# An image-token transformer block: the value projection's high and low weights side by side, in two banks

## The chip, the cores and the metric

The kernel runs on one core of one Trainium2 chip. The metric is the device time of one launch in microseconds (us). The text uses the engines' names: TensorE (PE in the rows; PEld for its weight loads), VectorE (DVE), ScalarE (ACT), GpSimd (POOL) and SyncE (SP), whose queue issues most transfers.

## What is computed

For each of 64 images of 3 x 224 x 224 a patch embedding with position codes, three layers of a graph convolution over a 28 x 28 grid and an output projection give 784 tokens of 64 features; 77 text tokens are joined to them, so that an image has 861 tokens. Then come attention with four heads of 16 features and a mixture of four experts, both behind a normalisation. Cut to what matters here:

```python
h = concatenate([tokens(x), txt], axis=1)                 # 64 x 861 x 64
a = layernorm(h)
q, k, v = heads(a @ Wq.T + bq), heads(a @ Wk.T + bk), heads(a @ Wv.T + bv)
out = softmax(q k^T / 4) v                                # per image and head
h = h + bf16(out) @ Wo.T + bo
h = h + shared_mlp(layernorm(h)) + top-2 of 4 experts, weighted
```

## The kernel before, in words

**Order of the work.** Everything after the setup is one list of steps (`window`, `image_steps`, `pair_steps`, lines 83 to 235). Each step has a due time in units of an image; all engines walk through the same list, sorted by due time, and each issues what its own branch of the step says. Work of several images overlaps: in the unit from g to g + 1 the scores of image g are formed (steps `s`, line 1121, and `pv`, line 1130), while the maxima of image g + 1 (`mx`, TensorE line 1142, VectorE line 894) and the experts of image g - 1 are worked on. `spread` divides the time between a start and an end over steps by their `COST`. The tables at lines 163 to 178 hold the starts and ends, one pair for even and one for odd images: `FINISH` (transposes of the attention output, line 1217, emptied at lines 995 and 996, and the output projection), `NORM_M` (normalisation ahead of the experts: its sum is line 946, its scaling line 965), `VALUE` (the value projection), `PACK`, `FETCH` and `LOAD_LEAD` (loading and packing of image columns, for SP and GpSimd) and more. The work of the graph convolution (`gw`, line 1169, low parts on VectorE at line 916; `gagg`, line 1178) is done for a pair of images, in the first half of each even unit. So a pair of images, an even and an odd one, is the period of the schedule. Sixteen pairs are laid out as one program window; the engines meet between windows.

**Banks.** PSUM has eight banks. Two hold the attention output (`pv`). The other six (0, 1, 2, 3, 6, 7) rotate: each step in `ROTATING` takes the next one, TensorE waits until the step six turns earlier has been emptied by its reader (semaphore `free`), and the reader waits for `full`. Each engine works in the order of the list, so a step that VectorE reads late holds its bank, and the turn six later waits on TensorE.

**Precision.** Weights and activations of some products are split into a high and a low part in fp32r. The token stack `x_stack_attn` (XS["a"], 128 rows: 64 features high, 64 low; 861 columns) is made by step `xt`. A product with the high weights (WH) and one with the low weights (WL), added in PSUM, give the value at nearly full precision.

**The value projection** (step `v`, TensorE lines 1198 to 1212, VectorE lines 982 to 989). An image has NB = 7 blocks of BLK = 123 tokens. For each block the tokens' 128 x 123 tile is the stationary operand, and the 64 columns of the value weights are streamed twice, high and low, into the same 64 columns of one bank:

```python
for k in range(NB):
    x_ = XS[which][:, k * BLK:(k + 1) * BLK]
    for part in (WH, WL):
        mm = pe.matmul(T[0:BLK, k * HID:(k + 1) * HID], x_, wsplit(part, "v"),
                       start=part is WH, stop=part is WL)
```

VectorE then adds the bias to all 7 x 64 columns in one operation and writes `v_and_one` (VV, two images deep), which the first `pv` of that image waits for. The gate's projection (step `gate`, line 1207) has its high and low weights side by side already, as `gate_hi_lo`. Semaphore `v_chain` orders VectorE's dependent operations (`done`, `need`, `settle`).

## Time and profile before

| | |
|---|---|
| times of three runs | 5132.30, 5137.61, 5141.29 us, median 5137.61 |
| the profiled execution | 5131.56 us, span 5129.8 us |
| mean granted TensorE clock | 0.968 of full speed |
| instructions in the span | 81306 |
| products and weight loads | 29710 each |
| DMA | 386.00 MB, mean 75 GB/s |

The first value projection starts some 235 us into the span: until then the setup, the first images' loading and the first graph layers run. The last stretch has the last images' experts. Between them the schedule repeats with each pair of images, and the two program windows that it fills differ little. In a row of the time line, a run of like instructions is merged: its start, the time from its first start to its last end, and behind it in brackets the idle time of the engine ahead of it and what ended that. A weight load of TensorE can run beside the product before it. The durations of products hold their latency, so their distance from start to start is shorter than the duration.

### The profile page before, as it was taken

The numbers are of one execution on the slowest core, as the hardware profiler recorded it, in microseconds if no ns is written. First come the engines' busy times: TensorE is split into PE (matmuls) and PEld (weight loads), VectorE is DVE, ScalarE is ACT, GpSimd is POOL, SyncE is SP. The second block draws the span as 40 slices with busy tenths as digits, with TensorE's granted clock in tenths as the row PEclk, the third lists the DMA queues.
The fourth block names the chain that finished last, engine by engine and source line by source line (L and its number), as shares of the span: only waits on it lengthen the run. The fifth ranks groups of instructions, "written<-read, shape, count | busy, mean of one in ns | idle before, by whom it ended". The sixth has DMA issues, their size and how long they took to land.

```text
span 5129.8 us, 81306 instructions
## 1 busy us (share of the span) xinstructions
PE 4804.8 (94%) x29710; PEld 3194.6 (62%) x29710; DVE 3517.5 (69%) x7660; ACT 2991.8 (58%) x6161; POOL 1268.7 (25%) x1169
## 2 busy tenths in 40 slices
PE   5389999999999999999999999999999999999998
PEld 4256666666666666666666666666666666666654
DVE  3167677777777776777776777777677777767774
ACT  0036666656666665666665665666566666666665
POOL 1113122222222222222221222222222222222121
PEclk8689999999999999999999999999999999999998
DMA  1332333343333243334333333324323332332220
GB/s 38 102 89 73 84 80 72 77 88 80 77 85 70 75 86 82 79 77 85 72 79 77 79 79 86 73 74 86 82 79 78 86 73 77 86 82 70 39 46 6
DMA packets 193397, 386.00 MB, mean 75 GB/s; under 512 B 74986, under 2 KB 118634, under 8 KB 193002
## 3 DMA queue, kind: packets, MB, share of 16 engines
q1 hardware_dynamic: 191978, 379.91, 33.2%
q8 instruction: 240, 3.93, 0.4%
q14 instruction: 155, 1.27, 0.1%
q10 hardware_dynamic: 1024, 0.89, 0.1%
HBM read 309.13 MB, written 109.26 MB: 82 GB/s over the span
## 4 chain that ended last, share of the span: by engine, by line
PE 55%; issue 22%; POOL 10%; DVE 6%; ACT 3%; DMA 2%; SPq 0%; POOLq 0%; ACTq 0%; DVEq 0%; another core or an unknown queue 0%
PE ps L1142 9%; PE ps L1121 8%; PE ps L1130 8%; PE ps L1178 8%; PE ps L1196 5%; PE ps L1169 4%; DVE neg_max_halves L894 3%; PE ps L1239 3%; POOL tokens L746 3%; POOL moe_T L741 2%; ACT probs L778 2%; PE ps L1260 2%; DMA image_rows<-image_by_row 2%; PE ps L1154 2%; POOL nodes_T L723 1%
## 5 line engine op out<-in xcount | busy, mean ns | idle before, releaser
L894 DVE TENSOR_REDUCE neg_max_halves<-ps 123x1 f32<-123x432 f32 (+1 forms) x3584 | 2016.6, 597 | 596.4 <-PE ps L1142 586.8
L778 ACT ACTIVATE probs<-ps 123x432 f32<-123x432 f32 x3584 | 1684.3, 541 | 602.2 <-PE ps L1121 579.8
L1142 PE MATMUL ps<-k_stack,q_stack 96*123 96x432 f32 x3584 | 1299.9, 396 | 37.3 <-DMA k_stack<-qk_scratch 22.3
L1121 PE MATMUL ps<-q_stack,k_stack 97*123 97x432 f32 x3584 | 1247.0, 394 | 64.5 <-DVE neg_max_halves L894 22.1
L1142 PEld LDWEIGHTS ps<-k_stack,q_stack 96*123 96x123 f32 x3584 | 644.1, 188 | 432.4 <-issue 289.5
L1121 PEld LDWEIGHTS ps<-q_stack,k_stack 97*123 97x123 f32 x3584 | 642.8, 186 | 360.2 <-issue 96.6
L1130 PE MATMUL ps<-probs,v_and_one 123*32 123x432 f32 x7168 | 787.7, 553 | 13.8 <-ACT probs L778 13.8
L841 ACT ACTIVATE hidden<-ps,plain_w 128x432 f32<-128x432 f32 x640 | 400.5, 634 | 182.0 <-PE ps L1196 181.9
L1178 PE MATMUL ps<-adjacency,parts_hi 112*128 112x392 f32 x1344 | 467.0, 347 | 5.3 <-DVE parts_lo L916 4.1
L1178 PE MATMUL ps<-adjacency,parts_lo 112*128 112x392 f32 x1344 | 461.7, 344 | 0.0
L711 POOL COPY patch_columns<-image_rows 96x392 f32<-96x392 f32 x256 | 238.3, 959 | 822.5 <-PE ps L1154 736.0
L1130 PEld LDWEIGHTS ps<-probs,v_and_one 123*32 123x32 f32 x7168 | 183.8, 111 | 373.6 <-issue 272.7
L727 POOL TENSOR_TENSOR ln_stats_m<-ln_stats_m,minus_half 123x7 f32<-123x7 f32 x64 | 95.1, 1485 | 1242.9 <-DVE ln_stats_m L960 1242.9
L741 POOL TENSOR_TENSOR moe_T<-gate_weights,bias_rows 123x448 f32<-123x448 f32 x256 | 254.1, 993 | 394.8 <-DVE gate_weights L1064 356.7
L723 POOL TENSOR_TENSOR nodes_T<-nodes_T,dinv_row 128x392 f32<-128x392 f32 x128 | 130.9, 1023 | 883.9 <-ACT nodes_T L790 883.9
L746 POOL TENSOR_TENSOR tokens<-tokens,moe_T 123x448 f32<-123x448 f32 x256 | 292.6, 1143 | 33.0 <-POOL moe_T L741 0.9
L1169 PE MATMUL ps<-plain_w,nodes_T 128*112 128x128 f32 (+2 forms) x1792 | 250.3, 279 | 31.4 <-POOL nodes_T L723 28.3
L785 ACT ACTIVATE parts_hi<-ps 112x512 fp32r<-112x512 f32 x192 | 104.9, 546 | 284.4 <-PE ps L1169 284.3
L847 ACT ACTIVATE hidden<-ps,plain_w 128x492 f32<-128x492 f32 (+1 forms) x384 | 234.1, 636 | 62.5 <-PE ps L1239 52.1
L1178 PEld LDWEIGHTS ps<-adjacency,parts_hi 112*128 112x128 f32 x1344 | 256.5, 191 | 18.3 <-DVE parts_lo L916 12.0
L1178 PEld LDWEIGHTS ps<-adjacency,parts_lo 112*128 112x128 f32 x1344 | 256.7, 191 | 1.4
L933 DVE TENSOR_TENSOR nodes_T<-ps,dinv_row 128x392 f32<-128x392 f32 x192 | 108.4, 565 | 209.7 <-PE ps L1178 207.6
(156 smaller groups left out, 6197.9 us busy)
## 6 DMA issues: line engine op xcount, KB each, us to landing
image_rows<-image_by_row SPq DMA_DIRECT2D x256, 586.9 KB
q_stack<-qk_scratch SPq DMA_DIRECT2D x256, 216.0 KB, 8.2
k_stack<-qk_scratch SPq DMA_DIRECT2D x256, 216.0 KB, 9.3
image_by_row<-in_x SPq DMA_DIRECT2D x192, 196.0 KB
qk_scratch<-parts_hi SPq DMA_DIRECT2D x64, 432.0 KB, 2.5
qk_scratch<-parts_lo SPq DMA_DIRECT2D x64, 432.0 KB, 3.2
out<-tokens SPq DMA_DIRECT2D x64, 215.2 KB
tokens_next<-in_txt SPq DMA_DIRECT2D x64, 19.2 KB
```

The costliest lines, as they stand in the source:

```text
L711: pool.tensor_copy(XCB[:, b, :, :].rearrange("p g (i j) -> p g i j", j=GRID), src).then_inc(xc_done, 1)
L741: ins = pool.tensor_tensor(TMP[:, :, :], GW[:, :, e:e + 1].to_broadcast(shape), row("eb3", e).unsqueeze(1).to_broadcast(shape), ALU.mult)
L746: ins = pool.tensor_tensor(hb, hb, TMP[:, :, :], ALU.add)
L778: act.activation(P[:, (g * 2 * NB + unit) % SLOTS, h, :], T[0:BLK, 0:HW], ACT.Exp, scale=SCALE).then_inc(free[r], 1)
L841: act.activation(H1[e % 3][:, c0:c0 + cn], T[:, 0:cn], ACT.Relu, bias=bias).then_inc(free[r], 1)
L894: v.tensor_reduce(NM[:, qb * HEADS + h, half:half + 1], T[0:BLK, 0:keys], AX.X, ALU.max, negate=True).then_inc(free[r], 1)
L1121: mm = pe.matmul(T[0:BLK, 0:cn], KS[:, g % 2, h, kb * BLK:(kb + 1) * BLK], QS[:, g % 2, h, c0:c0 + cn], start=True, stop=True)
L1130: pm = pe.matmul(acc[32 * h:32 * h + 32, half, 0:HW], VV[:, g % 2, kb, h, :], P[:, slot, h, :], start=kb == 0, stop=kb == NB - 1, tile_pos ...
L1142: mm = pe.matmul(T[0:BLK, 0:cn], QS[0:SHIFT_ROW, g % 2, h, qb * BLK:(qb + 1) * BLK], KS[0:SHIFT_ROW, g % 2, h, c0:c0 + cn], start=True, st ...
L1169: mm = pe.matmul(T[0:m, at * 128:(at + 1) * 128], HT[:, k * size:k * size + m], rhs, start=True, stop=True)
L1178: mm = pe.matmul(T[:, 0:GHALF], part[:, k, :], adj[:, k, half * GHALF:(half + 1) * GHALF], start=k == 0 and part is UH, stop=k == NG - 1 a ...
L1196: mm = pe.matmul(T[:, 0:cn], wsplit(part, name, e, cols), XS[which][:, c0:c0 + cn], start=part is WH, stop=part is WL)
```

## The change

The value weights' high and low parts are copied once, in the setup, into one tile of 128 columns (`v_hi_lo`). Each block now has one product of 128 columns, so that the high half and the low half lie side by side in PSUM. 7 x 128 columns don't fit into a bank of 512, so the step becomes two, `("v", g, 0)` with blocks 0 to 3 and `("v", g, 1)` with blocks 4 to 6, each with a bank and a turn of its own; the second is due VGAP = 0.163 after the first. VectorE adds bias and high half, and then, behind a wait on its own semaphore, the low half, for each of the two. The first product with the values waits for both. The cost of `v` goes from 7 to 3, and due times of `FINISH`, `NORM_M`, `BIAS`, `PROJECT`, `VALUE`, `PACK`, `FETCH` and `LOAD_LEAD` are changed. The gate's branch is written anew and does what it did.

```diff
--- before.py
+++ after.py
@@ -80,7 +80,7 @@
 STACK_PARTS = 8
 SLOTS = 3
 WAIT = 9
-COST = {"s": 1, "pv": 4, "mx": 1, "embed": 5, "gw": 5, "gagg": 12, "xt": 2, "qk": 2, "v": 7, "gate": 4, "l1": 2,
+COST = {"s": 1, "pv": 4, "mx": 1, "embed": 5, "gw": 5, "gagg": 12, "xt": 2, "qk": 2, "v": 3, "gate": 4, "l1": 2,
         "l2": 4, "wt": 2, "wb": 1, "l3": 12, "ot": 4, "obt": 2, "wo": 6, "back": 4, "mrow": 2}
 
 
@@ -161,21 +161,22 @@
 
 
 MAX = ((-0.693, 0.158), (-0.638, 0.167))
-FINISH = ((1.016, 1.084), (1.072, 1.145))
-NORM_M = ((1.109, 1.222), (1.167, 1.195))
+FINISH = ((1.002, 1.07), (0.994, 1.145))
+NORM_M = ((1.109, 1.222), (1.154, 1.195))
 EXPERT = ((1.374, 1.997), (1.267, 1.882))
 GATE = ((1.464, 1.665), (1.347, 1.379))
-BIAS = ((1.602, 1.743), (1.585, 1.71))
+BIAS = ((1.602, 1.743), (1.572, 1.71))
 NORM_A = ((-1.472, -1.34), (-1.672, -1.474))
-PROJECT = ((-1.307, -1.271), (-1.361, -1.284))
+PROJECT = ((-1.307, -1.281), (-1.361, -1.284))
 STACK = ((-1.043, -1.0), (-1.082, -0.936))
-VALUE = (-1.012, -0.998)
+VALUE = (-0.962, -0.984)
 
 GRAPH = (-2.077, -1.521)
-PACK = (-4.063, -3.676, -3.424, -2.795)
+PACK = (-4.053, -3.676, -3.424, -2.795)
+VGAP = 0.163
 STORE = (2.555, 2.602)
-FETCH = -5.76
-LOAD_LEAD, EMBED_LAG = 0.144, 0.217
+FETCH = -5.73
+LOAD_LEAD, EMBED_LAG = 0.133, 0.217
 
 
 def image_steps(g):
@@ -191,7 +192,7 @@
             + part(norm_steps(g, "m"), NORM_M) + part(expert_steps(g), EXPERT) + part(gate_steps(g), GATE)
             + part([("hb", g, n) for n in range(2 * EXPERTS + 1)], BIAS) + part(norm_steps(g, "a"), NORM_A)
             + part(project, PROJECT) + part([("stack", g, n) for n in range(STACK_PARTS)], STACK)
-            + [(g + VALUE[b], ("v", g)), (g + STORE[b], ("store", g))])
+            + [(g + VALUE[b], ("v", g, 0)), (g + VALUE[b] + VGAP, ("v", g, 1)), (g + STORE[b], ("store", g))])
 
 
 def pair_steps(p):
@@ -306,6 +307,7 @@
         ident_bf = sb("ident_bf", [128, 128], BF16)
         before = sb("before", [128, 16], F32)
         gsplit = sb("gate_hi_lo", [128, 2 * EXPERTS], F32R)
+        vsplit = sb("v_hi_lo", [128, 2 * HID], F32R)
         selcol = sb("expert_columns", [128, EXPERTS], F32)
         wo3 = sb("wo_parts", [65, 3, 64], BF16)
         posb = sb("pos_and_bias", [128, PATCHES], F32)
@@ -403,6 +405,8 @@
                     settle(v.tensor_tensor(WL[:, :], raw[:, :], WH[:, :].bitcast(F32), ALU.subtract))
                     v.tensor_copy(gsplit[:, 0:EXPERTS], wsplit(WH, "gW").bitcast(F32))
                     v.tensor_copy(gsplit[:, EXPERTS:2 * EXPERTS], wsplit(WL, "gW").bitcast(F32))
+                    v.tensor_copy(vsplit[:, 0:HID], wsplit(WH, "v").bitcast(F32))
+                    v.tensor_copy(vsplit[:, HID:2 * HID], wsplit(WL, "v").bitcast(F32))
                     sel = slice(SEL_ROW, SEL_ROW + 3 * EXPERTS)
                     settle(v.tensor_tensor(selcol[sel, :], ident[sel, SEL_ROW:SEL_ROW + EXPERTS],
                                            ident[sel, SEL_ROW + EXPERTS:SEL_ROW + 2 * EXPERTS], ALU.add))
@@ -980,13 +984,16 @@
                                                in1=QKH[:, c0:c0 + cn].bitcast(F32), op0=ALU.add, op1=ALU.subtract
                                                ).then_inc(free[r], 1)
                     elif kind == "v":
-                        b = st[1] % 2
+                        _, g, part = st
+                        ks = blocks_of(part)
+                        k, kn = slice(ks[0][0], ks[-1][0] + 1), len(ks)
                         v.wait_ge(full[r], n)
-                        v.tensor_tensor(
-                            VV[:, b, :, :, 0:HD],
-                            T[0:BLK, 0:NB * HID].rearrange("p (k h d) -> p k h d", h=HEADS, d=HD),
-                            row("bv").rearrange("p (h d) -> p h d", h=HEADS).unsqueeze(1)
-                            .to_broadcast([BLK, NB, HEADS, HD]), ALU.add).then_inc(free[r], 1)
+                        two = T[0:BLK, 0:kn * 2 * HID].rearrange("p (k a h d) -> p k a h d", a=2, h=HEADS, d=HD)
+                        bias = row("bv").rearrange("p (h d) -> p h d", h=HEADS).unsqueeze(1).to_broadcast([BLK, kn, HEADS, HD])
+                        done(v.tensor_tensor(VV[:, g % 2, k, :, 0:HD], two[:, :, 0, :, :], bias, ALU.add), st)
+                        need(st)
+                        v.tensor_tensor(VV[:, g % 2, k, :, 0:HD], two[:, :, 1, :, :], VV[:, g % 2, k, :, 0:HD], ALU.add
+                                        ).then_inc(free[r], 1)
                     elif kind == "ot":
                         ks = out_blocks(st[2])
                         k0, kn = ks[0], len(ks)
@@ -1123,7 +1130,8 @@
                     elif kind == "pv":
                         _, g, half, kb = st
                         if (half, kb) == (0, 0):
-                            emptied(pe, turn, ("v", g))
+                            emptied(pe, turn, ("v", g, 0))
+                            emptied(pe, turn, ("v", g, 1))
                         emptied(pe, turn, ("s", g, half, kb, HEADS - 1))
                         slot = (g * 2 * NB + half * NB + kb) % SLOTS
                         for h in range(HEADS):
@@ -1195,21 +1203,16 @@
                         for part in (WH, WL):
                             mm = pe.matmul(T[:, 0:cn], wsplit(part, name, e, cols), XS[which][:, c0:c0 + cn],
                                            start=part is WH, stop=part is WL)
-                    elif kind in ("v", "gate"):
-                        g = st[1]
-                        which = "a" if kind == "v" else "m"
-                        if kind == "gate":
-                            emptied(pe, turn, ("xt", g, "m", 0))
-                            emptied(pe, turn, ("xt", g, "m", 1))
+                    elif kind == "gate":
+                        emptied(pe, turn, ("xt", st[1], "m", 0))
+                        emptied(pe, turn, ("xt", st[1], "m", 1))
                         for k in range(NB):
-                            x_ = XS[which][:, k * BLK:(k + 1) * BLK]
-                            if kind == "gate":
-                                mm = pe.matmul(T[0:BLK, k * 2 * EXPERTS:(k + 1) * 2 * EXPERTS], x_, gsplit[:, :],
-                                               start=True, stop=True)
-                                continue
-                            for part in (WH, WL):
-                                mm = pe.matmul(T[0:BLK, k * HID:(k + 1) * HID], x_, wsplit(part, "v"),
-                                               start=part is WH, stop=part is WL)
+                            mm = pe.matmul(T[0:BLK, k * 2 * EXPERTS:(k + 1) * 2 * EXPERTS],
+                                           XS["m"][:, k * BLK:(k + 1) * BLK], gsplit[:, :], start=True, stop=True)
+                    elif kind == "v":
+                        for k, at in blocks_of(st[2]):
+                            mm = pe.matmul(T[0:BLK, at * 2 * HID:(at + 1) * 2 * HID],
+                                           XS["a"][:, k * BLK:(k + 1) * BLK], vsplit[:, :], start=True, stop=True)
                     elif kind == "ot":
                         _, g, part = st
                         emptied(pe, turn, ("pv", g, part, 0))
```

## Rows read from the trace of the kernel before

**Rows 1.** The page, busy time of each engine with its share and instructions.

```profile
PE 4804.8 (94%) x29710; PEld 3194.6 (62%) x29710; DVE 3517.5 (69%) x7660; ACT 2991.8 (58%) x6161; POOL 1268.7 (25%) x1169
```

**Rows 2.** Steady stage: us; busy PE, PEld, DVE, ACT, POOL (instructions); clock, DMA share, GB/s.

```profile
3000.00:4000.00 1000.00, 972.77 (x6104) 647.12 (x6106) 718.90 (x1564) 615.62 (x1270) 256.87 (x238) 0.99 0.36 80
```

**Rows 3.** The page, the chain that ended last, share of the span.

```profile
PE 55%; issue 22%; POOL 10%; DVE 6%; ACT 3%; DMA 2%; SPq 0%; POOLq 0%; ACTq 0%; DVEq 0%; another core or an unknown queue 0%
```

**Rows 4.** Waits of the weight loads in 3000 to 4000: in total, times, longest.

```profile
PEld ps L1121 <- DVE neg_max_halves L894: 17.1, 53, 0.8
PEld ps L1121 <- ACT probs L778: 15.0, 33, 0.9
```

**Rows 5.** Line 1211 alone: duration in ns min/median/max, first and last start.

```profile
L1211 PEld LDWEIGHTS ps<-split_hi,x_stack_attn x448: 182/188/330, 235.7 to 4967.0; 128*123 128x123 f32 x150
```

**Rows 6.** Instructions in order: start, duration of the run, engine, line (four groups of products).

```profile
4152.41 0.27 PE L1211 MATMUL ps<-split_lo,x_stack_attn 128*123 128x64 f32 x1
...
4153.70 0.27 PE L1211 MATMUL ps<-split_lo,x_stack_attn 128*123 128x64 f32 x1
...
3094.72 0.60 PE L1265 MATMUL ps<-ident_r,moe_T 128*123 128x128 f32 x4
...
3046.12 0.81 PE L1207 MATMUL ps<-gate_hi_lo,x_stack_moe 128*123 128x8 f32 x7
```

**Rows 7.** VectorE's groups: shapes, count | busy us, mean ns | idle before.

```profile
L985 DVE TENSOR_TENSOR v_and_one<-ps,bias_rows 123x448 f32<-123x448 f32 x64 | 39.4, 616 | 17.9 <-PE ps L1211 17.9
L946 DVE TENSOR_REDUCE ln_stats_m<-tokens 123x7 f32<-123x448 f32 x64 | 39.4, 615 | 0.1
...
L996 DVE TENSOR_TENSOR attn_bf<-ps,inv_sums 123x256 bf16<-123x256 f32 x64 | 27.2, 424 | 2.2
L1094 DVE TENSOR_TENSOR tokens<-ps,tokens 123x256 f32<-123x256 f32 x64 | 26.6, 416 | 16.0 <-PE ps L1265 16.0
L996 DVE TENSOR_TENSOR attn_bf<-ps,inv_sums 123x192 bf16<-123x192 f32 x64 | 22.9, 358 | 2.2
L1095 DVE TENSOR_TENSOR tokens<-ps,tokens 123x192 f32<-123x192 f32 x64 | 22.3, 348 | 0.0
...
L995 DVE RECIPROCAL inv_sums<-ps 123x16 f32<-123x16 f32 x64 | 16.1, 252 | 0.3
```

**Rows 8.** Instructions in order, an even image's value step at 4152.

```profile
4151.59 3.17 DVE L894 TENSOR_REDUCE neg_max_halves<-ps 123x1 f32<-123x429 f32 x6 [1.18 <-PE ps L1142]
...
4154.81 0.40 PEld L1217 LDWEIGHTS ps<-ident_r,attn_T 128*123 128x123 f32 x3 [0.33 <-DVE neg_max_halves L894]
...
4159.29 1.12 DVE L894 TENSOR_REDUCE neg_max_halves<-ps 123x1 f32<-123x432 f32 x2 [0.29 <-PE ps L1142]
```

**Rows 9.** Stretches of 5 us, columns as in rows 2.

```profile
4068.00:4073.00 5.00, 5.00 (x34) 4.95 (x34) 3.29 (x8) 1.33 (x3) 0.00 (x0) 1.00 1.06 124
...
4153.00:4158.00 5.00, 4.90 (x28) 3.41 (x26) 4.93 (x13) 2.48 (x5) 0.00 (x0) 1.00 1.04 120
4158.00:4163.00 5.00, 4.94 (x53) 3.18 (x53) 3.92 (x9) 3.19 (x6) 0.00 (x0) 1.00 1.04 113
...
4168.00:4173.00 5.00, 4.47 (x31) 2.52 (x29) 4.93 (x11) 3.71 (x8) 0.90 (x1) 1.00 0.14 40
```

**Rows 10.** Instructions in order, after the even image's value step, 4164 to 4171.

```profile
4164.97 0.18 PEld L1121 LDWEIGHTS ps<-q_stack,k_stack 97*123 97x123 f32 x1 [0.89 <-ACT probs L778]
...
4166.78 1.30 DVE L965 TENSOR_TENSOR centred_and_squared<-centred_and_squared,ln_stats_m 123x448 f32<-123x448 f32 x1 [1.60 <-POOL ln_stats_m L727]
...
4169.77 1.11 DVE L894 TENSOR_REDUCE neg_max_halves<-ps 123x1 f32<-123x432 f32 x2
...
4170.43 0.46 PE L1121 MATMUL ps<-q_stack,k_stack 97*123 97x432 f32 x1 [0.53 <-DVE neg_max_halves L894]
```

**Rows 11.** Instructions in order, after the odd image's value step at 4067.8.

```profile
4072.47 0.57 DVE L933 TENSOR_TENSOR nodes_T<-ps,dinv_row 128x392 f32<-128x392 f32 x1 [1.71 <-PE ps L1178]
...
4085.24 0.19 PEld L1178 LDWEIGHTS ps<-adjacency,parts_hi 112*128 112x128 f32 x1 [0.38 <-DVE parts_lo L916]
```

## The prediction

> **What bounds the kernel now.** I read the page's engine table first, then a table by stages, then the chain, the waits, and last the order of instructions around the two places that the change touches. TensorE is busy 4804.8 of 5129.8 us and VectorE 3517.5 [rows 1]. In a steady stage of 1000 us TensorE is at 973, VectorE at 719 and ScalarE at 616, at a granted clock of 0.99 of 2.4 GHz [rows 2]. The chain that ended last is 55% TensorE and 22% issue [rows 3]. So the kernel is bound by TensorE, but not at every moment: in that same stage the weight loads of the score products wait 17.1 us for VectorE's maxima and 15.0 us for ScalarE's exponentials [rows 4], as a new product may only start when one of six rotating banks is empty. The value projection runs 64 times, its first start at 235.7 us and the start of its last block at 4967.0 us [rows 5], which makes (4967.0 - 235.7) / 63 = 75.1 us for an image; this is also the length of one unit of due time.
>
> **What is removed from TensorE.** An image has 14 products of 64 columns now. From the second to the fourteenth start of one group it is 4153.70 - 4152.41 = 1.29 us for 12 steps, 0.1075 us each [rows 6], so 14 cost 1.51 us. The new product has 128 columns and the same stationary tile of 123. No row shows just that; the nearest are four fp32 products of 128 columns on 123, which take (0.60 - 0.27) / 3 = 0.11 us each (0.27 being the last one's own duration, taken from the value products), and seven of 8 columns on 123, (0.81 - 0.27) / 6 = 0.09 us [rows 6]. Eight, 64 and 128 columns cost about the same: the stationary tile sets the pace. I take 0.109 us: 7 products cost 0.76 us. TensorE is relieved of 0.75 us an image, 48 us in 64 images. The TensorE page of the Trainium skill (TensorE: Matmul & The Clock Gate, Back-to-back issue gap) speaks against the change: it counts some 60 cycles for up to 64 columns and 134 for 128. By it alone, 7 x 134 against 14 x 60 cycles, TensorE would pay 0.04 us more for each image; the row of the products of 128 columns is against that, and the rule is a rival below.
>
> **What is added to VectorE.** Now one addition of 448 elements takes 616 ns. The two parts have 256 and 192 elements and two additions each. Additions of these sizes from a bank take 416 and 348 ns, and a dependent one starts some 34 ns after the one before it (2.2 us over 64) [rows 7]. So part 0 costs 2 x 0.416 + 0.03 = 0.86 us, part 1 0.73 us, together 1.59 against 0.62: 0.97 us more an image, 62 us in all. This would be more than TensorE gains, were VectorE the bound; it counts only where VectorE has no idle time left.
>
> **Even images, part 0** (due 0.05 later than now, some 4 us; the finish of the image before is 0.014 earlier). Here VectorE starts six maxima at 4151.59 and next waits for TensorE at 4159.29, for 0.29 us; TensorE waits for a bank in between (0.33 us ahead of the transposes, the first of three such waits) [rows 8]. In 4153 to 4158 VectorE is busy 4.93 of 5 us, in 4158 to 4163 3.92 [rows 9]. Taking 1.51 us out of TensorE's queue here and putting 0.44 us back (4 x 0.109) gives at most 1.07 us. VectorE gets 0.86 - 0.62 = 0.24 us more in 10 us in which it has 5 + 5 - 4.93 - 3.92 = 1.15 us free, and that leaves at most 0.91 us. The lower end is a loss of 0.24 us, if its queue sets the pace throughout. I take a gain of 0.45 us, between the ends, as the first half of the stretch is full and the second isn't.
>
> **Even images, part 1** (0.163 after part 0, due 1.201). By the due times it falls between score products, at about 4165. There TensorE waits 0.89 us for ScalarE already [rows 10], and 3 x 0.109 = 0.33 us of products cost nothing; should that wait be gone, they cost 0.33 us. On VectorE the new step stands behind the scaling of the normalisation (line 965, due 1.193), which waits 1.60 us for GpSimd and starts at 4166.78. Behind it come the high and low parts, then the first maxima at 4169.77, and for these TensorE waits 0.53 us at 4170.43 [rows 10]. The 0.73 us are put into exactly this queue, in a window where VectorE is at 4.93 of 5 us [rows 9]. So the cost is between 0 (part 0 and the finish bring all of it forward) and 0.73 us; I take 0.50 us. An even image then comes out at about -0.45 + 0.50 = +0.05 us.
>
> **Odd images.** The window is full for TensorE (5.00 of 5) and not for VectorE (3.29) [rows 9]: after the value step it waits 1.71 us for the first aggregation [rows 11]. Part 0, and the two transposes that the new finish times (0.994 for 1.072) put ahead of that aggregation, can use this idle time: 0.24 us for part 0, and the four operations that empty the transposes, 1.28 us together (twice 0.25 at most, 0.42, 0.36 [rows 7]), are 1.52 us. The transposes also fill TensorE while it would wait for the low parts, so they cost nothing where they go, and their 1.1 us is missing where they were. The gain is 1.07 us. Part 1, due 0.179, goes ahead of an aggregation that waits 0.38 us for line 916 [rows 11]: 0.33 us of products fit. But the normalisation now starts at 0.154 in place of 0.167, ahead of that line 916 (due 0.157), and its first sum takes 0.62 us (line 946, [rows 7]): between 0 and 0.62 us are lost; I take 0.22 us, since the wait covers some. An odd image: -1.07 + 0.22 = -0.85 us, with ends of -1.07 and -0.45 us.
>
> **The small ones.** Two casts of 64 columns in the setup, once: less than two of the 0.62 us additions [rows 7], and at nothing, as TensorE counts the graph's edges beside them; uncovered 1.2 us. PACK, PROJECT, FETCH and LOAD_LEAD move their steps by 0.010 to 0.030, 0.8 to 2.3 us. SP's fetches and loads and GpSimd's packing go past a few stacks and score steps with them; a fetch is due 1.07 images, 80 us, before its first load, and GpSimd is at 257 of 1000 us [rows 2], so nothing; if a packing is late in each pair its embedding waits at most 0.8 us, 26 us in all. The wait of the first product with the values for part 1 is 0.8 of an image later than part 1, and covered. One more turn of the banks for each image comes at the price already counted, the bank held behind VectorE. The first and last 200 us are not counted.
>
> **The sum.** A pair of images: -0.85 + 0.05 = -0.80 us; 32 pairs: -26 us. The profiled execution took 5131.6 us, which becomes 5106; the median of the runs shown is 6 us above that execution, and against it I say 5111.
>
> **Rivals.** (1) **TensorE sets the pace everywhere**: -0.75 us x 64 = -48 us, from the median 5090; with part 1 hidden in waits, -1.07 x 64 = -68 us, 5069. For it is the busy share of 97%; against it are the waits of rows 8 and 10. (2) **The odd images' gain is eaten by the even ones**: even part 0 gives nothing and part 1 costs its 0.73 us; -0.85 + 0.73 = -0.12 us, -4 us, 5134. For it: VectorE is at 4.93 of 5 us at both even places. (3) **VectorE's queue becomes the bound** at the first maxima after the normalisation: even images lose 0.24 + 0.73 = 0.97 us, and odd ones lose their gain, as the transposes and part 0 (1.52 us) overrun the 1.71 us of idle time once this has shrunk by the 1.07 us that TensorE is earlier, and part 1 and the earlier sum cost 0.22 us net: +1.19 us a pair, +38 us, 5176. It decides once the maxima are later by more than the finish is earlier. Against it: VectorE is at 72% over the stage. (4) **A product of 128 columns costs twice one of 64**: 7 x 0.215 us are the 1.51 us of now, nothing is gained, and VectorE's terms (0.05 + 0.45 on even, 0.22 on odd images) stay: +0.72 us a pair, +23 us, 5161. This is the page's rule as rows price it. The 0.11 us of rows 6 speak against it.
>
> **The numbers.** My forecast 0.47, rival 1 0.25, rival 2 0.14, rival 3 0.11, rival 4 0.03. A measurement of this kernel can tell about 0.2% (10 us) from no change, so faster means under 5127, slower over 5148. Faster: the forecast, rival 1 and a little of rival 2's spread, 0.73; the same: rival 2, 0.13; slower: rivals 3 and 4, 0.14. The range leaves out rivals 3 and 4 and the far end of rival 1: 5078 to 5138.
>
> **What would show it.** In the profile after: products of line 1211's successor at 0.107 to 0.112 us from start to start (0.2 would be rival 4); VectorE's additions x256 of about 416 and 348 ns; TensorE's busy time lower by some 50 to 60 us; the wait for the first maxima in rows 10 longer by half a us on even images and none such on odd ones; distances between the odd and the next even value step shorter, and the other distance the same. Wrong I would be if the even images gain as much as the odd ones, or if waits for line 894 grow by over 1 us an image.

## The result, and the profile after

The changed kernel takes 5109.83 us (median of six runs, 5105.71 to 5111.67) against 5134.95 us for the kernel before (median of six, 5129.94 to 5141.29): a ratio of 0.9949 with a 95% interval of 0.9936 to 0.9961, or 25 us less. The forecast was 5111 us. The rest of this document shows that most of the gain of the profiled execution did not come the way that the forecast had it.

First the page of the changed kernel: busy time of each engine, and the chain that ended last.

```profile
PE 4797.5 (94%) x29262; PEld 3164.6 (62%) x29262; DVE 3520.8 (69%) x7854; ACT 3002.0 (59%) x6161; POOL 1268.7 (25%) x1169
...
PE 55%; issue 23%; POOL 8%; DVE 8%; DMA 3%; ACT 2%; SPq 0%; POOLq 0%; ACTq 0%; DVEq 0%; another core or an unknown queue 0%
```

Compared with [rows 1] and [rows 3], the weight loads are fewer by 448 (7 an image) as they should be, but TensorE's busy time fell by 7.3 us only, and VectorE's rose by 3.3 us, not by the 62 us that the forecast added. Next, the changed lines. They are from the table by line, the columns being those of [rows 7]:

```profile
L976 DVE TENSOR_TENSOR normed_hi_lo<-centred_and_squared,normed_hi_lo 123x448 fp32r<-123x448 f32 x128 | 88.0, 688 | 2.2
...
L973 DVE CAST normed_hi_lo<-centred_and_squared 123x448 fp32r<-123x448 f32 x128 | 68.8, 537 | 1.2
...
L995 DVE TENSOR_TENSOR v_and_one<-ps,v_and_one 123x256 f32<-123x256 f32 x64 | 27.2, 425 | 2.2
...
L993 DVE TENSOR_TENSOR v_and_one<-ps,bias_rows 123x256 f32<-123x256 f32 x64 | 26.8, 419 | 9.3 <-PE ps L1214 9.1
...
L995 DVE TENSOR_TENSOR v_and_one<-ps,v_and_one 123x192 f32<-123x192 f32 x64 | 22.9, 357 | 2.2
L993 DVE TENSOR_TENSOR v_and_one<-ps,bias_rows 123x192 f32<-123x192 f32 x64 | 22.2, 347 | 0.5 <-PE ps L1214 0.5
```

The four additions cost 425, 419, 357 and 347 ns, as the forecast had them; they are 99.1 us in place of the one addition's 39.4 [rows 7], 59.7 us more. But the two operations that split the normalised tokens (lines 973 and 976) have become cheaper. In the kernel before they were

```profile
L972 DVE TENSOR_TENSOR normed_hi_lo<-centred_and_squared,normed_hi_lo 123x448 fp32r<-123x448 f32 x128 | 116.9, 913 | 2.2
...
L969 DVE CAST normed_hi_lo<-centred_and_squared 123x448 fp32r<-123x448 f32 x128 | 80.3, 627 | 2.2
```

so 117 + 80 us became 88 + 69 us: 40 us of the added 60 came back here, 5.7 us in the scaling of the other normalisation (the one ahead of the attention, 68.4 to 62.7), and the rest but for the 3.3 in smaller amounts elsewhere. What made these operations cheaper is seen further down.

**Where the 22 us between the two profiled executions come from** is read best from one step that every image has, the first product of the output projection. Its starts in even images mark the pairs. Three of the kernel before, then five of the changed one, from the time line:

```profile
3409.07 1.36 PE L1228 MATMUL ps<-wo_parts,attn_bf_T 65*123 65x64 bf16 x21
...
3558.87 1.36 PE L1228 MATMUL ps<-wo_parts,attn_bf_T 65*123 65x64 bf16 x21
...
3709.24 1.36 PE L1228 MATMUL ps<-wo_parts,attn_bf_T 65*123 65x64 bf16 x21
```

```profile
380.46 1.34 PE L1231 MATMUL ps<-wo_parts,attn_bf_T 65*123 65x64 bf16 x21
...
529.06 1.34 PE L1231 MATMUL ps<-wo_parts,attn_bf_T 65*123 65x64 bf16 x21
...
679.08 1.34 PE L1231 MATMUL ps<-wo_parts,attn_bf_T 65*123 65x64 bf16 x21
...
3236.25 1.34 PE L1231 MATMUL ps<-wo_parts,attn_bf_T 65*123 65x64 bf16 x21
...
3386.45 1.34 PE L1231 MATMUL ps<-wo_parts,attn_bf_T 65*123 65x64 bf16 x21
```

The pairs of the kernel before took 149.80 and 150.37 us; those of the changed one 148.60, 150.02 and 150.20 us. The table by stages gives the granted clock of the same pairs (it is the number ahead of the DMA share; the others as in [rows 2]):

```profile
3409.00:3559.00 150.00, 145.84 (x920) 96.89 (x919) 108.69 (x239) 93.32 (x193) 39.07 (x36) 1.00 0.36 80
3559.00:3709.00 150.00, 145.81 (x916) 96.84 (x915) 108.25 (x238) 92.70 (x193) 39.02 (x36) 0.99 0.36 80
```

```profile
380.00:529.00 149.00, 145.34 (x906) 95.58 (x905) 108.81 (x245) 93.52 (x194) 38.98 (x36) 1.00 0.35 79
529.00:679.00 150.00, 146.28 (x904) 96.20 (x902) 108.63 (x244) 93.48 (x193) 39.01 (x36) 0.99 0.36 80
3236.00:3386.00 150.00, 146.52 (x903) 97.05 (x902) 108.53 (x244) 93.47 (x192) 39.02 (x36) 0.98 0.36 80
```

Where the clock stays at 1.00 the change has shortened the pair by 1.20 us. Where it doesn't, by 0.17 us. And in the changed kernel only two of 31 pairs (0 and 16, counted from 0) have a clock of 1.00 throughout. In 27 others it falls to 0.50 (1.2 of 2.4 GHz) for 3 to 7 us behind the same work; in the other two (15, where the program windows meet, and 30, with the last images) it falls for 10 us elsewhere. This is pair 19:

```profile
3353.00:3358.00 5.00, 4.56 (x25) 1.97 (x27) 4.47 (x8) 3.30 (x8) 4.59 (x4) 0.98 0.27 103
3358.00:3363.00 5.00, 5.00 (x22) 3.51 (x15) 4.89 (x10) 1.06 (x2) 3.52 (x4) 0.50 0.26 105
3363.00:3368.00 5.00, 5.00 (x21) 2.93 (x20) 2.24 (x4) 2.26 (x4) 0.00 (x0) 0.84 0.31 124
```

```profile
3354.93 0.36 PE L1150 MATMUL ps<-k_stack,q_stack 96*123 96x432 f32 x1
3355.22 1.09 PE L1254 MATMUL ps<-image_rows 12*128 12x492 bf16 x3
3356.55 0.33 PE L1254 MATMUL ps<-image_rows 12*128 12x369 bf16 x1 [0.24 <-DVE neg_max_halves L898]
3356.81 2.21 PE L1138 MATMUL ps<-probs,v_and_one 123*32 123x432 f32 x16
3358.95 1.44 PE L1150 MATMUL ps<-k_stack,q_stack 96*123 96x432 f32 x3
```

Ahead of the fall TensorE issues the four select products of an odd image (line 1254, two for each of the two column ranges). Each works on 12 of 128 rows, and they wait for VectorE and ScalarE between one another; then come the products with the values. The fall begins 2.5 us behind the start of the first select product in pairs 17 to 28, and 6 to 7 us behind it in pairs 1 to 14. The kernel before has a stretch at 0.50 by the same products in 26 of 31 pairs, and five pairs of 151.2 to 153.2 us (0, 6, 7, 9, 14), in three of which a second or a longer one falls. The lengths of the pairs, marked in this way, add up as follows: 21 regular pairs (1 to 5, 10 to 13, 17 to 28) gained 2.7 us in all, seven others (0, 6 to 9, 14, 16) gained 12.6 us, the pair with the change of the program window 4.7 us (161.0 to 156.3), and the start 2.5 us; the last images give the rest, some 0.4 us of loss. Of the 12.6 us, 11.0 are those of the five pairs of over 151 us. So half of the gain of this execution came from five pairs in which the kernel before had been slowed more than usual. Three of the regular pairs (20, 23, 27) had a clock of 1.00 before and lost 0.4 us each, since they have a stretch at 0.50 after.

### The profile page after: what moved, and what is told of

The parts are those of the page before. It is cut to its first block, busy times and chain, and to the rows that moved or that the text cites. A ratio compares the mean times of both kernels' runs of the same rounds, so it can differ in the third digit from the quotient of the medians.

```text
span 5107.7 us, 80667 instructions
## 1 busy us (share of the span) xinstructions
PE 4797.5 (94%) x29262; PEld 3164.6 (62%) x29262; DVE 3520.8 (69%) x7854; ACT 3002.0 (59%) x6161; POOL 1268.7 (25%) x1169
## 4 chain that ended last, share of the span: by engine, by line
PE 55%; issue 23%; POOL 8%; DVE 8%; DMA 3%; ACT 2%; SPq 0%; POOLq 0%; ACTq 0%; DVEq 0%; another core or an unknown queue 0%
PE ps L1186 9%; PE ps L1138 9%; PE ps L1128 9%; PE ps L1150 8%; PE ps L1204 5%; DVE neg_max_halves L898 4%; PE ps L1177 3%; POOL tokens L750 3%; PE ps L1242 3%; POOL moe_T L745 2%; DMA image_rows<-image_by_row 2%; PE ps L1263 2%; PE ps L1192 2%; PE ps L1162 1%; ACT probs L782 1%
## 5 line engine op out<-in xcount | busy, mean ns | idle before, releaser
L1138 PE MATMUL ps<-probs,v_and_one 123*32 123x432 f32 x7168 | 762.7, 539 | 2.0 <-ACT probs L782 2.0
L750 POOL TENSOR_TENSOR tokens<-tokens,moe_T 123x448 f32<-123x448 f32 x256 | 304.1, 1188 | 37.3 <-POOL moe_T L745 0.9
L851 ACT ACTIVATE hidden<-ps,plain_w 128x492 f32<-128x492 f32 (+1 forms) x384 | 234.2, 636 | 62.7 <-PE ps L1242 52.3
```

The source lines that it names most:

```text
L750: ins = pool.tensor_tensor(hb, hb, TMP[:, :, :], ALU.add)
L1138: pm = pe.matmul(acc[32 * h:32 * h + 32, half, 0:HW], VV[:, g % 2, kb, h, :], P[:, slot, h, :], start=kb == 0, stop=kb == NB - 1, tile_pos ...
```

## The experiments

Two theories stood against one another: that the queues alone set the pace, as in the prediction, and that the stretches at 0.50 take back what a faster pair gains. The ratios are to runs of the kernel before made beside them, with medians of 5130.8 to 5135.6 us.

**New due times alone, e1_times_only.** The kernel before with the new tables:

```diff
-FINISH = ((1.016, 1.084), (1.072, 1.145))
+FINISH = ((1.002, 1.07), (0.994, 1.145))
-VALUE = (-1.012, -0.998)
+VALUE = (-0.962, -0.984)
...
```

> The kernel before with only the new due times (FINISH, NORM_M, BIAS, PROJECT, VALUE, PACK, FETCH, LOAD_LEAD); the value step is one bank with 14 narrow products, as before. Queue theory (the steps of the prediction: each pair of images is shorter by what the queues give, and stretches at the lower clock are a constant): the earlier transposes and the earlier sum shift waits only, a pair without a stretch at the lower clock takes 149.8 us as before, give or take 0.3, and the time is that of before within 8 us. Clock theory (a stretch at a granted clock of 0.5 once in each pair gives back what a faster pair gains, and most of the 25 us come from irregular stretches that the change happens to remove): the same 149.8 us for an undisturbed pair, but the time can be up to 20 us below that of before if the irregular stretches of two or more at 0.5 in one pair go away with the new times alone.

5222.3 us, ratio 1.0167 (1.0150 to 1.0185): 87 us slower, which neither theory had. Most of its pairs take 153.6 us, from 3459.17 to 3612.79 here, with two places where the clock falls. One is by the odd images' select products. The other is a value step, the odd image's in pairs 12, 13 and 16 to 28 (at 3520.58 here, with the fall 1.7 us behind its start), and the even image's in pairs 2 to 8:

```profile
3459.17 1.34 PE L1228 MATMUL ps<-wo_parts,attn_bf_T 65*123 65x64 bf16 x21
...
3612.79 1.34 PE L1228 MATMUL ps<-wo_parts,attn_bf_T 65*123 65x64 bf16 x21
```

```profile
3517.00:3527.00 10.00, 8.97 (x49) 8.26 (x48) 6.03 (x15) 2.44 (x6) 0.00 (x0) 0.83 1.05 118
3585.00:3592.00 7.00, 6.89 (x27) 4.45 (x27) 5.45 (x11) 2.72 (x5) 2.09 (x2) 0.76 0.25 101
```

Its only pair without such a stretch took 150.6 us. By this one pair the due times cost some 0.8 us a pair by their order, and the rest up to 153.6, 3 us, comes with the stretches at 0.50.

**The split with the old due times, e2_split_old_times.** The changed kernel with the tables of before.

```diff
-VALUE = (-0.962, -0.984)
+VALUE = (-1.012, -0.998)
...
```

> The changed kernel with the due times of before (the first part of the value step due at -1.012 and -0.998, the second 0.163 later; v costs 3). Queue theory: on odd images the first aggregation now waits for the low parts, so 0.5 of the 1.07 us are gained there, even images give nothing: -0.3 to -0.5 us a pair against before, some 5120 to 5127 us. Clock theory: an undisturbed pair is shorter than 149.8 us by 0.5 to 1.2 us, but the pairs with a stretch at 0.5 stay at 150.2 to 150.4 us, and the time lies between 5110 and 5135 depending on the irregular stretches only.

5155.2 us, ratio 1.0038 (1.0023 to 1.0054). Neither theory had that: the split alone is slower, though TensorE has 448 products less. Its pairs mostly go round in threes of 152.2, 151.2 and 150.6 us, the last without a stretch at 0.50. So each half of the change costs 0.8 us a pair at full clock, and together they gain 1.2 us.

**Full products by the select products, e3_full_products_at_select.**

```diff
+                        if g % 2:
+                            pe.matmul(T[:, 0:HW], wsplit(WH, "sW1"), XS["m"][:, 0:HW], start=True, stop=True)
                         mm = pe.matmul(T[:, 0:cn], select[...], GT[:, c0:c0 + cn], start=True, stop=True, ...)
```

> The changed kernel with one extra product of 128 rows and 432 columns into the same bank ahead of each of the four select products (12 rows) of odd images; the real product writes over it. Queue theory: four more products of 0.2 us each in a stretch where TensorE also waits: +0.2 to +0.8 us a pair, +6 to +26 us, 5116 to 5136. Clock theory: the granted clock falls to 0.5 right behind these select products because they keep few rows of the array at work; with full products among them it stays at 1.0 in most pairs, a pair takes 148.6 + 0.2 to 0.8 = 148.8 to 149.4 us in place of 150.2, and the time falls by 20 to 40 us, to 5070 to 5090.

5104.72 us, ratio 0.9941 (0.9926 to 0.9956). Eight of the 31 pairs now keep the clock at 1.00. Seven of them take 148.6 us in spite of four more products, which go into waits; the eighth is pair 29 near the end, with 146.95 us. The others, but for one where the windows meet and one at the end, fall as before and take 150.1 to 150.2 us. So the full products can keep the clock up, as the clock theory has it, but the time lies 15 us over its range, as most pairs still fall.

**Two narrow products a block, e4_two_narrow_products.**

```diff
-mm = pe.matmul(T[0:BLK, at * 2 * HID:(at + 1) * 2 * HID], XS["a"][...], vsplit[:, :], start=True, stop=True)
+for half in range(2):
+    c = at * 2 * HID + half * HID
+    mm = pe.matmul(T[0:BLK, c:c + HID], XS["a"][...], vsplit[:, half * HID:(half + 1) * HID], start=True, stop=True)
```

> The changed kernel with two products of 64 columns a block, side by side, in place of one of 128: TensorE does the 14 products of before, VectorE and the banks are as changed. Queue theory: TensorE gives back 0.75 us on each image less what waits hide (part 1 of both images is hidden, 0.33 us each), so +0.84 us a pair, +27 us, about 5137. Clock theory: the pairs are held at 150.2 us by the stretch at 0.5, so half or more of that is not seen, and the time rises by less than 14 us unless the irregular stretches of before come back.

5129.36 us, ratio 0.9987 (0.9977 to 0.9998), 19.5 us over the changed kernel, between the two. Regular pairs with a stretch at 0.50 take 150.3 us against 150.2: there 7 products on each image cost next to nothing. The one regular pair without took 149.72 us against 148.60. The remainder is four irregular pairs, of 151 to 153 us, that came back (9 us), a longer change of the window (3.9 us) and pair 16 (1.7 us), which had a clock of 1.00 in the changed kernel; the start (2.9 us more) and the end (3.4 us less) nearly cancel.

**Two full products, e5_two_full_odd**, the same edit as e3 with two in place of one.

> The changed kernel with two full products (128 rows, 432 columns) ahead of each select product of odd images. With one of them (the run before) the pairs without a stretch at 0.5 still took 148.6 us, so the products fit into waits, and 8 of 31 pairs had no such stretch. Clock theory: with two, nearly no pair has a stretch at 0.5; pairs take 148.6 to 149.2 us, and the time is 5065 to 5085 us. Queue theory (the clock is no lever): the time stays at 5100 or rises by up to 0.4 us a select product, 51 us.

5089.06 us, ratio 0.9918 (0.9896 to 0.9940). The clock is at 1.00 in all steady pairs and falls only where the program windows meet and at the ends. Two marks and the clock between them:

```profile
3223.08 1.34 PE L1231 MATMUL ps<-wo_parts,attn_bf_T 65*123 65x64 bf16 x21
...
3372.39 1.34 PE L1231 MATMUL ps<-wo_parts,attn_bf_T 65*123 65x64 bf16 x21
```

```profile
3223.00:3372.00 149.00, 145.51 (x911) 96.01 (x909) 108.44 (x243) 93.01 (x192) 39.04 (x36) 1.00 0.35 80
```

A pair takes 149.2 to 149.3 us, 0.7 more than the 148.6 of e3: so the second four products are no longer hidden by waits. This is the clock theory's result, 4 us over the upper end of its range; the queue theory's 5100 or more is out.

**Both parities, e6_two_full_all**, without the condition on g.

> The same with the two full products in even images too. The stretches at 0.5 of the steady part stand at one place of the pair, by the odd images' select products, and so the even ones' should change nothing in the clock: the pair is longer than with odd ones alone by 0 to 1.6 us, as far as waits don't hide them. If the clock falls at the even ones' place once it no longer falls at the odd ones', this kernel is the faster of the two.

5164.35 us, ratio 1.0061 (1.0041 to 1.0081); a pair takes 151.5 us at a clock of 1.00. The even images' eight products cost 2.2 us, over the range that I gave. The 0.2 us that I had for one of them was too small; in even images they stand as

```profile
3010.70 0.66 PE L1255 MATMUL ps<-x_stack_moe,split_hi 128*128 128x432 f32 x2
3011.29 0.38 PE L1256 MATMUL ps<-image_rows 12*128 12x492 bf16 x1
```

so two take 3011.29 - 3010.70 = 0.59 us, eight 2.4 us, and nearly all of it shows. There is no fall at their place to prevent.

**The kernel before with the same products, e7_before_two_full_odd.**

> The kernel before with the two full products in odd images. It measures the change without the clock: pairs at full clock took 149.8 us before and 148.6 us after. Clock theory: this kernel has few stretches at 0.5 as well, a pair takes 149.8 to 150.2 us, the time is 5105 to 5120 us, and it lies above that of the changed kernel with the same products by 1.2 us x 31 = 37 us. If the gain of the change lay only in stretches at 0.5 that went away, the two would be within 10 us.

5125.16 us, ratio 0.9987 (0.9978 to 0.9996). The time is 5 us over the range. All its steady pairs have a clock of 1.00 and take 150.3 us. So with the clock out of the way the change is worth 150.30 - 149.27 = 1.03 us a pair, and the medians differ by 36 us.

**One addition, e8_two_full_one_add**, e5 without the second addition, so that the low half is left out.

```diff
-done(v.tensor_tensor(VV[:, g % 2, k, :, 0:HD], two[:, :, 0, :, :], bias, ALU.add), st)
-need(st)
-v.tensor_tensor(VV[:, g % 2, k, :, 0:HD], two[:, :, 1, :, :], VV[:, g % 2, k, :, 0:HD], ALU.add).then_inc(free[r], 1)
+v.tensor_tensor(VV[:, g % 2, k, :, 0:HD], two[:, :, 0, :, :], bias, ALU.add).then_inc(free[r], 1)
```

> The changed kernel with two full products in odd images and only one addition on VectorE for each part of the value step: the low half isn't added. VectorE is relieved of 0.43 + 0.36 us and the waits between, 0.85 us an image. By the prediction's steps it costs 0.5 us on even images (the first maxima behind the normalisation) and nothing on odd ones: a pair is 0.5 us shorter than with both additions, 16 us in all. If VectorE's added work is free everywhere: the same within 3 us. If VectorE sets the pace at both places: 1.5 us a pair, 46 us.

5089.21 us, against 5089.06 with both: VectorE's second addition is free at these due times. The first additions, 0.42 and 0.35 us, stay in this run, and it doesn't price them. The busy times of VectorE with and without it (first e5's page, then this kernel's) and this kernel's line of the cast:

```profile
PE 4781.0 (94%) x29518; PEld 3159.6 (62%) x29518; DVE 3522.9 (69%) x7854; ACT 2991.5 (59%) x6161; POOL 1268.7 (25%) x1169
```

```profile
PE 4780.5 (94%) x29518; PEld 3165.3 (62%) x29518; DVE 3484.8 (68%) x7726; ACT 2990.0 (59%) x6161; POOL 1269.2 (25%) x1169
```

```profile
L973 DVE CAST normed_hi_lo<-centred_and_squared 123x448 fp32r<-123x448 f32 x128 | 81.9, 640 | 1.2
```

The 128 additions took 50.1 us (64 at 424 and 64 at 357 ns). VectorE's busy time is lower by 38.1 only, as the cast of the normalised tokens is up at 640 ns from 545 in e5, 12 us in all: a part of what the additions save is lost again in the cast behind them. The 38 us that are saved only become idle time of VectorE's, since the total doesn't follow.

**The mixture, e9_full_mixed**: two full products ahead of the first and third select product, one ahead of the others (`range(1 if t else 2)`).

> The changed kernel with full products ahead of the select products of odd images: two ahead of the first and third, one ahead of the second and fourth (six in all). With four a pair without a stretch at 0.5 took 148.6 us but 22 of 31 pairs had such a stretch; with eight no steady pair had one and a pair took 149.27 us. Clock theory: with six a pair takes 148.7 to 149.1 us; if no steady pair has a stretch at 0.5 the time is 5070 to 5084 us, below all others; if many have, it is 5095 to 5105 us, as with four.

5079.02 us, ratio 0.9895 (0.9873 to 0.9916), which beats both kernels: 52 us under the kernel before, and, by the ratios to it, some 28 us under the changed one. Steady pairs keep a clock of 1.00 and take 148.8 to 149.0 us.

**Old times at full clock, e10_split_old_times_full**, e2 with the full products of e5.

> The split value step with the due times of before, and the eight full products in odd images, so that the clock stays up. Its pairs without a stretch at 0.5 took 150.6 us without the full products, 0.8 us more than before's, and I put the cost in the order of the work by the odd and the even value step. If it is the order: a pair takes 150.3 + 0.8 = 151.1 us, the time is 5145 to 5155 us. If it was the clock: near the 149.27 us of the changed kernel, 5090 to 5100 us.

5186.05 us, ratio 1.0114 (1.0082 to 1.0146), slower than e2, which I had not expected: the fall at the select products is gone, but in about half of the pairs the clock now falls 147 to 155 us behind the mark, from 3 us behind the start of the next even image's value step on. The pairs at 1.00 take 151.1 to 151.2 us, as expected. So the order costs 0.86 us a pair against the 150.30 of e7, without any clock in it.

**New times alone at full clock, e11_times_only_full**, e1 with them.

> The kernel before with only the new due times, and the eight full products in odd images. Without them nearly every pair had two stretches at 0.5 and took 153.6 us; the one pair that had none took 150.6 us. If the loss of 87 us was mostly clock: a pair takes 150.3 + 0.8 = 151.1 us or a little more and the time falls from 5222 to 5145 to 5165 us. The full products stand at one of the two places only, so if the other stretch (by the even images' value step) stays, a pair takes 152 to 153 us, and the time is 5180 to 5210 us.

5204.27 us, ratio 1.0139 (1.0115 to 1.0162), in the second of the cases: the stretch by the select products went away, those by the value steps stayed. The expectation speaks of the even images' value step alone; the falls here are by the even images' step in most of the disturbed pairs and by the odd images' in seven. Disturbed pairs of the steady part take 151.7 to 156.3 us. Pairs at 1.00 take 151.3 to 151.4 us.

**Narrow products at full clock, e12_narrow_full**, e4 with them.

> The changed kernel with two products of 64 columns a block and the eight full products in odd images. It prices TensorE's share alone at full clock: the pair without a stretch at 0.5 was 149.72 us with narrow products and 148.60 with wide ones. Expected: 149.27 + 1.1 = 150.4 us a pair, 5089 + 35 = 5124 us. If the wide products' gain were hidden by waits as my prediction had it for part 1: 149.27 + 0.84 = 150.1 us, 5115 us. If all of it shows: +1.5 us, 5135 us.

5131.58 us, ratio 0.9996 (0.9985 to 1.0007). The time is between the two expectations of 5124 and 5135 us. A pair takes 150.44 us, 1.17 more than with wide products, near the 1.12 that the one pair of e4 had told. Two of its pairs still have a stretch at 0.50, elsewhere, and take 152.0 us.

The pairs at a clock of 1.00 and with the eight full products make a table that the totals don't show:

| | narrow products, one bank | two banks, wide products | two banks, narrow products |
|---|---|---|---|
| old due times | 150.30 (e7) | 151.16 (e10) | |
| new due times | 151.35 (e11) | 149.27 (e5) | 150.44 (e12) |

## Why the forecast came out, and what of it was wrong

**TensorE's term** held. The four products of part 0 and the three of part 1 are in the trace as

```profile
3084.80 0.65 PE L1214 MATMUL ps<-v_hi_lo,x_stack_attn 128*123 128x128 f32 x4
...
3091.92 0.54 PE L1214 MATMUL ps<-v_hi_lo,x_stack_attn 128*123 128x128 f32 x3 [0.53 <-ACT probs L782]
```

so (0.65 - 0.28) / 3 = 0.12 us each; from start to start, over all images, the median is 0.107 and the mean 0.112 us, by the 0.109 of the forecast, and not 0.2: rival 4 is out. The table by columns of the Trainium skill's page (TensorE: Matmul & The Clock Gate, Back-to-back issue gap), which the page gives for isolated products and not for a stream of weight loads and products, doesn't hold for these. Wide for narrow products is worth 1.17 us a pair (e12 against e5) of the 1.50 that I counted. The difference of 0.33 is the three products of part 1 in even images, which stand in a wait for ScalarE, as forecast: the 0.53 us ahead of them in the row above are that wait. Counted between the same score products in both traces, the odd image's place has 0.72 us of it and the even one's 0.45. So in odd images part 1's products weren't hidden, which the forecast had fit into a wait of 0.38 us. TensorE's busy time was to fall by 50 to 60 us and fell by 7.3 in the two profiles; at full clock, between e12 and e5, it is 4828.6 against 4781.0, 47.6 us, the 48 us of the forecast. The changed kernel spends more of its time at 0.50 (185 us against 162 behind the first mark), where products take longer (the 16 products with the values shown above take 2.21 us there and 1.66 in e5).

**Even images, part 1**: the forecast's 0.50 us of loss behind the normalisation was wrong. The place is right, the mechanism isn't: nothing is lost there. These are VectorE's and GpSimd's rows in the order of time, of the kernel before, and then of the changed one with the first score product behind them and with the same cast in the next image:

```profile
4166.71 2.20 POOL L711 COPY patch_columns<-image_rows 96x392 f32<-96x392 f32 x2
...
4168.12 1.08 DVE L969 CAST normed_hi_lo<-centred_and_squared 123x448 fp32r<-123x448 f32 x1
...
4169.23 0.63 DVE L972 TENSOR_TENSOR normed_hi_lo<-centred_and_squared,normed_hi_lo 123x448 fp32r<-123x448 f32 x1
```

```profile
3093.67 2.16 POOL L715 COPY patch_columns<-image_rows 96x392 f32<-96x392 f32 x2
3093.74 1.29 DVE L969 TENSOR_TENSOR centred_and_squared<-centred_and_squared,ln_stats_m 123x448 f32<-123x448 f32 x1 [1.60 <-POOL ln_stats_m L731]
...
3094.96 0.34 DVE L993 TENSOR_TENSOR v_and_one<-ps,bias_rows 123x192 f32<-123x192 f32 x1
...
3095.34 0.36 DVE L995 TENSOR_TENSOR v_and_one<-ps,v_and_one 123x192 f32<-123x192 f32 x1
...
3095.61 0.51 DVE L973 CAST normed_hi_lo<-centred_and_squared 123x448 fp32r<-123x448 f32 x1
...
3096.15 0.62 DVE L976 TENSOR_TENSOR normed_hi_lo<-centred_and_squared,normed_hi_lo 123x448 fp32r<-123x448 f32 x1
...
3097.35 0.46 PE L1128 MATMUL ps<-q_stack,k_stack 97*123 97x432 f32 x1 [0.35 <-DVE neg_max_halves L898]
```

```profile
3166.83 0.42 DVE L973 CAST normed_hi_lo<-centred_and_squared 123x448 fp32r<-123x448 f32 x1
```

Before, scaling (4166.78, [rows 10]) and cast ran beside GpSimd's packing copy; the cast took 1.08 us. Now the two additions stand between them, which read the bank and take 0.34 and 0.36 us beside the same copy, their usual time; when the cast comes the copy is nearly done, and it takes 0.51 us. With GpSimd idle, as on the next image (the last row), it takes 0.42. From the start of the scaling to the end of the low parts it is 4169.86 - 4166.78 = 3.08 us before and 3096.77 - 3093.74 = 3.03 us after. Of the 0.73 us, 0.57 are what the cast no longer loses, and the rest is overlap, as the first addition and the cast begin before the operation ahead of them has ended. This holds over the images: from the scaling's start to the low parts' end it is 3.06 us before and 3.07 us after on the mean of 28 even images. In e8, with one addition less, it is 3.08 us, since the cast begins earlier and takes 0.93 us: the end goes with GpSimd's copy and not with the additions. In all three kernels the cast ends 0.29 us behind the end of the second copy, within 0.01 us on the mean of those images, though it begins 0.78 us ahead of that end before, 0.22 after and 0.64 in e8. So it waits for the copy rather than running slower by a share. The wait for the first maxima, 0.53 us in [rows 10], is 0.35 us (at 3097.35); I had it growing by half a us.

**Odd and even images.** At full clock (e5 against e7, starts of the same score products) the odd images' place gives 0.7 us a pair and the even images' 0.36 us. The forecast had 0.85 and a loss of 0.05. Within the ends given there both lie, and the sum of 1.03 compares with 0.80: the term that was mis-sized is VectorE's 0.50 us for part 1 on even images, which measures nothing.

**The new due times** I took as a help at one place (the transposes ahead of the aggregation) and as small otherwise. The table says that they decide as much as the split: without them the split loses 0.86 us a pair, and on their own they lose 1.05. With them in place the split and the wide products are worth 151.35 - 149.27 = 2.08 us. Why the split loses with the old ones was not settled. Between e10 and e7, in pairs at a clock of 1.00, the loss stands in the first third of the even image's unit, behind the odd image's value step (0.54 us), and at the even image's value step (0.25 us). Nor is it shown which of the eight tables matters, as all of them were moved together.

**What the forecast left out is the clock.** It had the 0.99 of [rows 2] as a constant. In the profiled execution the regular pairs gained 0.1 to 0.2 us and not 0.8, since those of the changed kernel are held at 150.2 us by the stretch at 0.50. What made up for that were the seven pairs outside the regular run (12.6 us, 11.0 of them in pairs that had been irregular), the window change and the start (7.1 us), none of which had a term. With the forecast's own -0.80 for 31 pairs being -25 us, the total was met by terms that it didn't have: that it came within 1 us is luck. Whether the gain is made up the same way in the other five runs isn't known, as only one execution of each was profiled; the medians with the full products (36 us between e7 and e5, 25 without them) say that the clock takes back some 11 us of the change on the whole.

**The signs given.** The distance from the odd to the next even value step was to be shorter; from first product to first product its median went from 84.6 to 87.5 us, and the other from 65.8 to 62.7. The even images' step itself was put 0.05 later, so this sign could not tell what it was meant to.

**Rivals.** At full clock the change is worth 36 us, between the forecast's 26 and rival 1's 48 (TensorE everywhere). Rivals 2 and 3 rested on VectorE's queue, and e8 and the rows above speak against that. With the old due times the sign of rival 3 came true (e2), but no run shows that VectorE was the reason.

**What stays open.** That the full products keep the clock at 1.00 is shown (e3, e5, e9, and e7 for the kernel before). Why is not: each is a product on all 128 rows and also fills a wait, and no run had the one without the other, or put such products elsewhere to keep off another stretch.

## What to carry to other kernels

In a schedule that repeats, read the granted clock repeat by repeat: compare the repeats in which it stays at 1.00, and count the others apart. A few full-array products in a stretch of waiting products on few rows can be worth as much as the rewrite of a step (e9 gains some 28 us over the changed kernel, the change itself 25), where they fit into waits; where they don't, they cost their full time (e6). Moving an operation and its due times is one change: neither half of this one would have been kept by itself.

## What the runs showed that was not expected

- A regular pair of the changed kernel takes 150.2 us both where the stretch at 0.50 is 3.4 us long (pairs 6 to 14) and where it is 6.8 us (pairs 17 to 28), and 148.6 us without. The pace doesn't follow the length of the stretch. In such a row of pairs the fall comes at the same place of each (126.0 us behind the mark in pairs 6 to 14, 121.5 in 17 to 28). The pairs of e1 are held in the same way at 153.6 us, which is 3.4 us more, as long as the shortest stretch at 0.50. How the chip picks the pace isn't shown by these runs.
- Four full products more on each pair shorten it from 150.2 to 148.6 us in the pairs where the clock then stays up (e3).
- Taking one stretch away can bring up another: e10 has them by the even images' value step, where e2 had none in its steady pairs.
- A cast of 448 elements on VectorE takes 0.40 to 0.43 us where GpSimd is idle (37 of 128 in the trace before, 67 after), and up to 1.09 us beside GpSimd's work; the scaling takes 0.63 and 1.30 us. The 128 additions of 192 elements that read a PSUM bank don't change: all take 0.34 to 0.36 us, 91 of them wholly beside GpSimd's work.
